# A gated recurrence, its step ordered anew: the candidate right behind the first gates, the second layer's gate last, its tanh and x + h one step on

## The reference, cut to what matters

```
z  = sigmoid(x_t W_z + h U_z + vz)          # vz, vr, vh: constants of the condition
r  = sigmoid(x_t W_r + h U_r + vr)
hh = tanh(x_t W + (r * h) U + vh)
h  = (1 - z) * h + z * hh                   # layer 1;  x1 = x + h

gate = sigmoid(h1 Wh^T + x1_t Wz^T + b)
h1   = tanh(h1 * leak + gate * x1_t)        # layer 2;  x2 = x1 + h1
```

## Time and profile before

| | us |
|---|---|
| median of three runs | 986.1 (985.35 to 988.47) |
| the profiled execution: span | 989.0 |
| TensorE busy | 943.0 (95%) |
| TensorE weight loads busy | 766.4 (77%) |
| VectorE busy | 802.5 (81%) |
| ScalarE busy | 647.3 (65%) |
| GpSimd busy | 221.2 (22%) |

### The profile page before, as it was taken

One profiled execution on the slowest core, in us unless ns is written; L12 is line 12 of the kernel. 1 busy time (PEld: TensorE's weight loads), 2 busy tenths in 40 slices (PEclk: granted clock), 3 DMA queues, 4 the chain that ended last, 5 costly groups with the idle time before them and its releaser, 6 DMA issues.

```text
span 989.0 us, 112546 instructions
## 1 busy us (share of the span) xinstructions
PE 943.0 (95%) x50966; PEld 766.4 (77%) x50966; DVE 802.5 (81%) x2372; ACT 647.3 (65%) x2862; POOL 221.2 (22%) x430
## 2 busy tenths in 40 slices
PE   6699999999999999999999999969999999999996
PEld 5699999999999999999999998335555555555554
DVE  2378778878788778777878787799999999999992
ACT  2478777777777777777777776336455556555552
POOL 0011111111111111111111111324434334434340
PEclk7699999999999999999999999979999999999998
DMA  6113312310010100100101001100011000001001
GB/s 218 41 55 112 110 50 95 111 35 27 24 37 24 37 24 27 34 27 24 37 24 37 24 27 33 28 1 25 24 37 34 24 24 24 24 31 41 24 24 43
DMA packets 38294, 42.01 MB, mean 42 GB/s; under 512 B 5120, under 2 KB 31232, under 8 KB 37120
## 3 DMA queue, kind: packets, MB, share of 16 engines
q1 hardware_dynamic: 36832, 40.55, 13.2%
q10 hardware_dynamic: 1440, 1.18, 0.4%
HBM read 32.80 MB, written 8.91 MB: 42 GB/s over the span
## 4 chain that ended last, share of the span: by engine, by line
PE 57%; DVE 29%; issue 7%; ACT 4%; DMA 1%; ACTq 1%; POOL 0%; DVEq 0%; POOLq 0%
PE bank L788 30%; PE bank L734 22%; DVE arena L667 10%; DVE early L686 4%; DVE early L677 4%; ACT cand_kept L391 2%; DVE early L690 2%; DVE early L684 2%; DVE early L671 2%; DVE early L665 2%; DVE none_h L604 2%; PE bank L906 2%; PE bank L923 1%; DMA bias<-in_bias 1%; PE bank L877 1%
## 5 line engine op out<-in xcount | busy, mean ns | idle before, releaser
L734 PE MATMUL bank<-x_ahead,early 128*32 128x64 f32 x12376 | 345.7, 224 | 5.9 <-ACT bank L358 3.2
L734 PEld LDWEIGHTS bank<-x_ahead,early 128*32 128x32 f32 x12376 | 239.7, 111 | 3.3 <-issue 3.3
L788 PE MATMUL bank<-none_h,early 128*32 128x32 f32 x16384 | 203.1, 199 | 8.8 <-issue 4.9
L280 POOL TENSOR_TENSOR x<-x_f,h_gx 128x64 f32 x256 | 87.6, 342 | 529.4 <-PE bank L788 528.3
L788 PEld LDWEIGHTS bank<-none_h,early 128*32 128x32 f32 x16384 | 180.6, 110 | 27.4 <-DVE none_h L604 13.5
L906 PE MATMUL bank<-x,wl 128*128 (+1 forms) x384 | 182.3, 614 | 0.9 <-DVE rank_rows L646 0.9
L788 PE MATMUL bank<-rh_f,early 128*32 128x32 f32 x8192 | 151.0, 199 | 5.0 <-DVE rh_f L592 2.2
L906 PEld LDWEIGHTS bank<-x,wl 128*128 128x128 f32 x384 | 69.2, 192 | 89.0 <-issue 89.0
L788 PEld LDWEIGHTS bank<-rh_f,early 128*32 128x32 f32 x8192 | 122.1, 112 | 7.0 <-DVE rh_f L592 5.0
L604 DVE TENSOR_TENSOR_SCAN none_h<-zero_z,cand_kept 128x64 f32<-128x64 f32 x512 | 121.6, 279 | 5.3 <-ACT cand_kept L391 3.9
L402 ACT ACTIVATE h_gx<-h_pre 128x64 f32<-128x64 f32 x256 | 68.7, 268 | 81.0 <-DVE h_pre L630 81.0
(11 more groups left out here) (95 smaller groups left out, 1294.4 us busy)
## 6 DMA issues: line engine op xcount, KB each, us to landing
x_in<-in_x SPq DMA_DIRECT2D x34, 256.0 KB, 2.7
x_ahead<-in_x SPq DMA_DIRECT2D x130, 64.0 KB, 1.8
arena<-in_w SPq DMA_DIRECT2D x8, 1024.0 KB, 5.6
out<-y SPq DMA_DIRECT2D x32, 256.0 KB, 2.5
rank_rows<-in_bias_rows SPq DMA_DIRECT2D x1, 1024.0 KB, 5.0
arena<-scratch SPq DMA_DIRECT2D x64, 16.0 KB
early<-in_cx SPq DMA_DIRECT2D x1, 768.0 KB, 4.5
early<-in_wx SPq DMA_DIRECT2D x1, 768.0 KB, 6.3
```

The costliest lines, as they stand in the source:

```text
L280: pool.tensor_tensor(x2[:, :, :, s], x1_f[:, u % LOOP], h1_gx[:, u % 2, :, :, 0], ALU.add).then_inc(x2_done, 1)
L734: mm = pe.matmul(out[32 * j:32 * j + 32], weights(k, j, m), moving(k), start=False, stop=False, tile_position=(0, 32 * j), skip_group_chec ...
L788: mm = pe.matmul(out[32 * j:32 * j + 32], weights(k, j, m), moving(k), start=False, stop=k == 1, tile_position=(0, 32 * j), skip_group_che ...
```

## The change

On TensorE a step becomes: first gates, wide quarters, the candidate's four quarters in one piece, the second gate, wide quarters. Before it was: first gates, the second gate, the candidate with a wide quarter in its middle, wide quarters. ScalarE takes the second layer's tanh (`second_state`) of one step later, behind r and in front of z, and the gate's sigmoid behind the candidate's tanh. VectorE takes x + h of the step before behind r * h, and gate * x1 and the second layer's scan last. x_in waits for keep * h (`kept_done`), which stands behind the last x + h that reads it. Wide products of r and the candidate wait for their seeds by a semaphore of their own (`reset_seeded`), those of layer 2 for `x1_ready`. SyncE's last turn stands outside its loop.

```diff
             def next_steps(n, s):
-                sp.wait_ge(x1_done, n * BODY + (s + 1) * SLOT + 1)
+                sp.wait_ge(kept_done, 2 * (n * BODY + (s + 1) * SLOT + 1))
...
             def turn(n, first=False):      # ScalarE
                 for u in range(BODY):
                     second = not first or u >= LAG
-                    gates_first(n, u)
+                    reset(n, u)
+                    if not first or u > LAG:
+                        second_state(n, u)
+                    elif u:
+                        act.activation(idle[:, u - 1:u], var_eps[:], ACT.Copy).then_inc(h1_done, 1)
+                    update(n, u)
+                    candidate(n, u)
                     if second:
                         second_gate(n, u)
-                    candidate(n, u)
...
-                    if second:
-                        second_state(n, u)
...
             def turn(n, first=False):      # VectorE
                     reset_state(n, u)
+                    if first and u == 0:
+                        dve.memset(idle[:, LAG:LAG + 1], 0.0).then_inc(x1_ready, STEPS)
+                    elif u == 0:
+                        first_output(n - 1, BODY - 1)
+                    else:
+                        first_output(n, u - 1, first)
+                    kept_state(n, u)
+                    next_state(n, u)
                     if second:
                         second_gated(n, u)
-                    next_state(n, u)
-                    if second:
                         second_sum(n, u)
-                    first_output(n, u, first)
...
-            def first_cand(u, hole):
+            def first_cand(u):
                 pe.wait_ge(rh_done, 1)
                 cand(0, 0)
-                hole()
                 pe.wait_ge(rh_done, 2)
...
+            def second_inputs(at, par):
+                pe.wait_ge(x1_ready, STEPS)
+                ahead_second(at, par).then_inc(x1_ready, -STEPS)
+
+            def even(u):
+                par, nxt = u // STEPS, 1 - u // STEPS
+                first_gates(u, inputs=lambda: ahead_first(par, 1, 1).then_inc(ahead_loaded[par], -16))
+                pe.wait_ge(ahead_loaded[nxt], 16)
+                pe.wait_ge(reset_seeded, 2)
+                ahead_first(nxt, 0, 0).then_inc(reset_seeded, -2)
+                first_cand(u)
+                second_gate(u)
+                second_inputs((LOOP - STEPS, 0)[par], nxt)
+
+            def odd(u):
+                nxt = 1 - u // STEPS
+                first_gates(u)
+                ahead_first(nxt, 0, 1)
+                ahead_first(nxt, 2, 0)
+                first_cand(u)
+                second_gate(u)
+                ahead_first(nxt, 2, 1)
+                ahead_first(nxt, 1, 0)
...
             def turn():                    # TensorE
-                first_gates(3)
-                ahead_first(0, 2, 0, (0,))
-                second_gate(3)
-                first_cand(3, hole=lambda: ahead_first(0, 2, 0, (1,)))
-                ahead_first(0, 2, 1)
-                ahead_first(0, 1, 0)
-                ahead_first(0, 1, 1, (0,))
+                even(0)
+                odd(1)
+                even(2)
+                odd(3)
```

More of the change, by code:

```diff
@@ L215, in next_turn @@
                                  ).then_inc(ahead_loaded[c % 2], 16)
-                    if c == 6:
+                    if c == 6 and not last:
                         next_steps(n, 0)
@@ L219, in next_turn @@
                         sp.dma_start(dst, src).then_inc(done, 16)
-                next_steps(n, 1)
+                if not last:
+                    next_steps(n, 1)
             next_turn(0, [(dst[:], io[name], tail_in) for dst, name in TAIL_LOADS])
@@ L225, in _ @@
                 next_turn(w + 1, [(w2[w][:, s], io["w2"][:, w, s], w2_in[w]) for s in range(2)])
-            with sp.Fori(5, TURNS) as n:
+            with sp.Fori(5, TURNS - 1) as n:
                 next_turn(n)
+            next_turn(TURNS - 1, last=True)
             sp.wait_ge(rows_done, 4)
@@ L422, in turn @@
                         seed_gate(((u - LAG) // STEPS) % 2)
-                    if second:
-                        second_state(n, u)
-                    else:
-                        act.activation(idle[:, u:u + 1], var_eps[:], ACT.Copy).then_inc(h1_done, 1)
                     if first and u == LAG:
@@ L592, in reset_state, with kept_state @@
                     dve.tensor_tensor(rh_f[:, m], r_f[:, m], none_h[:, now, m, :, 1], ALU.mult).then_inc(rh_done, 1)
+            def kept_state(n, u):
+                t, now = n * BODY + u, (u + 1) % 2
                 dve.wait_ge(z_done, 2 * t + 2)
@@ L605, in next_state, with first_output @@
                                            0.0, ALU.mult, ALU.add).then_inc(h_done, 1)
-            def first_output(n, u, first):
+            def first_output(n, u, first=False):
                 t, nxt, slot = n * BODY + u, u % 2, u // SLOT
@@ L612, in first_output @@
                     dve.wait_ge(x2_done, t - LOOP + 2)
-                if not first or u >= LAG:
-                    dve.wait_ge(pre1_done, t - LAG + 1)
-                else:
-                    dve.memset(idle[:, LAG + u:LAG + u + 1], 0.0).then_inc(scanned, 1)
-                    dve.wait_ge(scanned, u + 1)
                 dve.tensor_tensor(x1_f[:, u % LOOP], x_in[:, slot, u % SLOT], none_h[:, nxt, :, :, 1],
-                                  ALU.add).then_inc(x1_done, 1)
+                                  ALU.add).then_inc(x1_ready, 1)
             def second_gated(n, u):
@@ L651, in _ @@
                 turn(n)
+            dve.wait_ge(pre1_done, T - LAG)
+            first_output(TURNS - 1, BODY - 1)
             dve.wait_ge(tail_in, 16 * len(TAIL_LOADS))
@@ L747, in ahead_second @@
                 for m in range(HALVES):
-                    ahead(pre_g[par][:, m].rearrange("p v b -> p (v b)"), m, col(wz1),
-                          lambda k: x1_f[:, at:at + STEPS, k, :])
+                    mm = ahead(pre_g[par][:, m].rearrange("p v b -> p (v b)"), m, col(wz1),
+                               lambda k: x1_f[:, at:at + STEPS, k, :])
+                return mm
             col = lambda w: (lambda k, j, m: w[:, k, j, m * BLK:(m + 1) * BLK])
@@ L771, in _ @@
             pe.wait_ge(wx_in, 16)
-            pe.wait_ge(seeded, 3)
-            for gate, m in ((0, 0), (0, 1), (2, 0), (2, 1)):
+            pe.wait_ge(seeded, 1)
+            pe.wait_ge(reset_seeded, 2)
+            ahead_first(0, 0, 0).then_inc(reset_seeded, -2)
+            for gate, m in ((0, 1), (2, 0), (2, 1), (1, 0)):
                 ahead_first(0, gate, m)
-            ahead_first(0, 1, 0)
-            ahead_first(0, 1, 1, (0,)).then_inc(ahead_loaded[0], -16)
             pe.wait_ge(hidden_in, 16 * len(HIDDEN_LOADS))
@@ L792, in quarter, with first_gates @@
                 return mm
-            def first_gates(u, late_keep=None):
+            def first_gates(u, inputs=None):
                 par, v, now = u // STEPS, u % STEPS, (u + 1) % 2
@@ L807, in first_gates @@
                 keep(1, 0)
-                mm = keep(1, 1)
-                if late_keep:
-                    mm = late_keep()
-                mm.then_inc(z_pre, 1)
+                if inputs:
+                    inputs()
+                keep(1, 1).then_inc(z_pre, 1)
             def second_gate(u, sums=None):
```

42 lines of the change are left out of this document (12 added, 30 removed).

## The result

The changed kernel takes 1000.7 us (median of 4 runs, 1000.07 to 1002.13), the kernel before 986.0 in the same job (985.35 to 988.47): ratio 1.014, 95% interval 1.0122 to 1.0158. The forecast was 981.0, with 971 to 992 as range. The profiled execution spans 1000.3 us against 989.0, and these 11.3 us are what the traces can explain.

The account below looks back on a forecast made before the run. TensorE was taken to wait on a chain through ScalarE and VectorE that closes on itself. A turn of 8.92 against 9.01 saves 5.5 us over 61 loops, less 0.4 at the end: 981.0 us, range 971 to 992.

Parts of the forecast that it names:

- r ahead of the second tanh, c = 1.20: In every step, c (load of the second candidate quarter) comes 1.20 us after T0 (first `none_h` load), not 1.26.
- it has none: TensorE has no backlog at T0: its loads from c on take 0.91 us, under the chain's 0.95 to 0.97.
- the backlog rival: TensorE comes to T0 still full of wide products, c 1.24 in three of four steps: 988.3 us; chance 0.20.
- Even steps, z "hidden, by 0.1": z follows the second tanh at 1.03 to 1.08; keep*h is done near 1.70, wanted at 1.80: no cost.
- The loop's end, "T0 = c + 1.23": In the loop's last step, last load 0.91 after c, plus the branch's 0.32: the step takes 2.43 against 2.34.
- my sign for it, the wait growing from 0.22 to 0.30: TensorE's `none_h` wait at its loop's end, seen 61 times, should grow from 0.22 to about 0.30 us.
- Turn of ScalarE's and VectorE's loops: Falling behind seeds and scan, the turn's 0.25 us once in 16 steps is covered: 0.06 per loop saved.
- VectorE's order, GpSimd beside it, SyncE: The second scan frees VectorE at T0 + 0.74, before r*h at 0.79; x_ahead lands 5.02, wanted 5.05: no cost.
- The rival that came nearest in size (993.8): VectorE and POOL collide in the chain, the next r*h 0.07 late in three of four steps: 993.8 us; chance 0.15.
- Start and end, 0.4: Before the loop nothing; behind it the first h1 tanh starts 0.36 later, on the path: 0.4 us lost.
- the forecast turn of 8.92: One four-step TensorE loop turn: steps of 2.17, 2.15, 2.17 and 2.43, 8.92 us against 9.01 before.

Follow-up runs that it names:

- e1_pad: The changed kernel with 12 more matrix products of zeros in its start-up, which shifts the code: 995.8 us, ratio to before 1.0084.
- e3_z_early: The changed kernel with the update gate's second-half input products moved into the odd step before, swapped with those of r's second half: 996.3 us.
- e4_short_end: The changed kernel with one wide quarter of each odd step moved from behind the second gate to ahead of the candidate: 1001.5 us.
- experiments 4 to 8: Four changed kernels with wide quarters moved ahead of the candidate (991.5 to 1001.5 us), and one with GpSimd's add on one of 32 columns (1004.2 us).
- e6_both: The changed kernel with 5 wide quarters ahead of the candidate in every step, 2 behind the gate in odd steps, 8 more start-up products: 996.0 us.
- experiments 11 and 12: The kernel before with only ScalarE's and VectorE's loop turns moved (987.1 us), then also three semaphore increments more in VectorE's start-up (984.5 us, ratio 0.9959).
- e7_short_end_pad: e4_short_end with the 12 start-up products of zeros of e1_pad: 991.5 us, ratio 1.0044.
- experiment 5: e1_pad with GpSimd's add computing only one of 32 columns of the x2 sum, x2 cleared first: 1004.2 us, its turn 9.104 against 9.112.
- e2_before_pad: The kernel before with 56 more matrix products of zeros in its start-up, which shifts the code: 1003.0 us, ratio 1.0151.

## Why the prediction was wrong, step by step

The chain of a step is the one that the prediction described, but it took TensorE to have no backlog, z to be hidden and the loop's end to be fixed behind the last load, and none of the three held. Each was worth a few hundredths a turn, all on the same side, and one loss of 4.8 us was not in the sum.

- *r ahead of the second tanh, c = 1.20.* Right in direction: nothing stands before r. But c is 1.217 to 1.229. In step 1, which starts from a standstill, the excess of 0.03 is the border 15 loads in (1.199 without it, in e1_pad). In the other three it is backlog: the step that failed is "it has none". It rested on 7 narrow quarters from a standstill in 0.46 and 32 wide loads in 0.45, 0.91 in all; behind c the same loads end at 0.955 (7 narrow quarters alone take 0.54: from 306.86 + 1.22 to 308.62). So T0 follows the last load by 0.02 behind the first odd step and by 0.05 behind even ones, and r starts at 0.58 to 0.59. Nor does a queue that is empty for 0.04 start fresh, as I held against the backlog rival: r starts 0.62 behind T0 when T0 follows the last load by 0.005 (e3_z_early), 0.59 to 0.61 at 0.02 (both), 0.583 at 0.045 (the changed kernel), 0.569 at 0.070 and 0.564 at 0.091 (e4_short_end, where c of that last one is 1.199). Cost against the forecast: 0.09 a turn, 0.06 of it backlog and 0.03 the border. The rival *Backlog stays* had this mechanism, with c at 1.24; its 988.3 lacks the terms that follow.
- *Even steps, z "hidden, by 0.1".* Failed. I took z from the tanh before it; in even steps it waits for the keep quarter behind two wide ones, and comes at 1.11 where I had 1.03 to 1.08. The scan is some 0.07 late, the step 0.03 longer behind c. Experiment 3 shows that curing it buys nothing: the bound behind it is TensorE. The second parts of the two even and the first odd step are 0.02 to 0.03 over the forecast each: 0.08 a turn.
- *The loop's end, "T0 = c + 1.23".* Too small: 1.272. The 0.32 behind the last load came out here (0.317), and the last load was 0.045 later. But that it is a fixed time behind the last load failed: with fewer wide quarters it grows to 0.41, and fixed is the 0.36 behind the branch's own record (experiments 4 to 8). Before and after agree in it because both have four or five wide quarters there, so the right value is in part luck. And my sign for it, the wait growing from 0.22 to 0.30, was wrong: the row counts only what follows the last load's end, and with four wide quarters behind the gate that is 0.21 although the last load is later; it grows, to 0.25 and 0.29, where they are fewer (e4_short_end, e6_both). The step lost 0.146 against before, not 0.09. The rule of the Trainium skill ("Advanced Engine Details and Errata", Sequencer and Instruction Queues: about 108 ns for a compare-and-branch) would have made it shorter still; the traces have 0.36 from the start of the branch's record to the next turn's first load in both kernels, and a median of 0.22 for the record itself.
- *Turn of ScalarE's and VectorE's loops.* Right: 0.06 a turn, confirmed by itself in experiments 11 and 12 (2.7 and 3.2 us of 3.7).
- *VectorE's order, GpSimd beside it, SyncE.* Right: no step of the changed kernel waits for them by more than 0.01, and the scan beside GpSimd takes 0.42 for 0.40. The margin is thin, as forecast: where r comes earlier (step 3 of e4_short_end and e7_short_end_pad) the first r*h follows it by 0.27 instead of 0.23, behind the second scan, and c is at most 0.01 late by it. The rival that came nearest in size (993.8) is refuted as a mechanism by experiment 5.
- *Start and end, 0.4.* Failed: 5.2. The later tanh is there (idle 1.11 where 0.88 stood), but the border of the code costs 2.9 and the clock behind it 1.5, and nothing in my sum stood for either. Even without the border (e1_pad) this stretch is 1.1 longer than before; 0.7 of that I can't assign.

Sum: the forecast turn of 8.92, plus 0.09 (c) and 0.12 (behind c, the loop's end among it), is 9.13, as measured. In spans the forecast was 5.1 less and the outcome 11.3 more. Of these 16.4, 13.9 are in the recurrence (8.4 + 5.5), 4.8 behind it (5.2 - 0.4), and 2.3 came back in the first steps and in layers 3 and 4. (Between the medians it is 19.7: the forecast took the span of before as 0.3% above its median, and that of after lies 0.4 us below its own.)

What the change of order did to a turn of 9.007: the hidden turns -0.06, earlier c in the other three steps -0.11, later second parts of steps 1 to 3 +0.08, the border +0.03, and the loop's end +0.19, because four narrow quarters more and one wide less stand there behind the candidate. The hidden turns, the border and the wide quarters at the loop's end were each tried by a run; r ahead of the second tanh, and the gate behind the candidate, were never tried alone, so their two terms are read from the traces of whole steps.

## What to carry to other kernels

Where an engine's queue is never quite empty, a quarter moved behind a milestone is paid there (here between half of its loads' time and all of it), and a gain at one wait returns as backlog at the next: add up the loads of a step before counting on a gap. Look at what a loop's branch has in front of it, on every engine, and turn loops where the engine waits anyway; that was the one part of this change that paid when it was made alone. And when a time moves by a few microseconds at a place that has no releaser, shift the code by a few instructions before explaining it by the order.

## What the runs showed of the hardware

- TensorE stops for 0.9 to 3.9 us when it first reaches certain places of its program. These lie every 128 loads (64 products), and move with the instructions ahead of them (experiments 1, 2). VectorE lost 2.8 us in the same way at one place, and three instructions ahead of it removed it (experiment 12). That it is the fetch of code is my reading; what is shown is that the place in the program decides.
- Six such blocks in a loop run without stops from the second turn on, twelve stop at each: 987 or 991 us became 1940.
- A border 15 loads behind a loop's start costs 0.03 to 0.13 in each turn; with the border 23 loads in (e2_before_pad, step 1) it is 0.015.
- The first load behind a branch of TensorE's loop started 0.353 to 0.364 us behind the start of the branch's record, whatever stood in front of it (all twelve kernels with a four-step loop).
- After 3 us of idleness TensorE's granted clock was at its lower level for 3.4 us (in the changed kernel from 624.4, in e2_before_pad from 626.2).
- A GpSimd add of 2 columns instead of 64 still takes 0.20 instead of 0.33.
